# Maxima per half of the keys, the next context split in eight pieces, and the probabilities' low part in thirds, in a two-attention program on one core

## What is computed

```
x = x + tanh(g_xattn[0]) * L0_xattn(layernorm(x), ctx, ctx, Wq, Wk, Wv, Wo)   # 16 heads
x = x + tanh(g_ffn[0])   * L0_ffn(layernorm(x), w1, conv_w, conv_b, w2)
x = x + tanh(g_xattn[1]) * L1_xattn(layernorm(x), ctx, mask, Wq, Wkv, Wo)     # 8 heads
x = x + tanh(g_ffn[1])   * L1_ffn(layernorm(x), w_gate, w_up, w_down)
# an attention: q, k, v by projection; softmax(q k / sqrt(d)) v per head; projection
```

## Time and profile before

| | us |
|---|---|
| median of 3 runs | 2538.94 (2537.11 to 2543.28) |
| profiled execution, its own time | 2547.8 |
| its span, first to last instruction | 2546.0 |
| first attention | about 0 to 850 |
| first feed-forward | about 850 to 1210 |
| second attention | about 1210 to 2005 |
| second feed-forward | about 2005 to 2546 |

### The profile page before, as it was taken

How to read it: one execution, slowest core, us unless ns; L and a number is a source line. 1 busy time by engine, 2 the same in 40 slices (tenths; PEclk the granted TensorE clock), 3 DMA queues, 4 the chain that set the end, 5 groups by cost and what they waited for, 6 DMA issues and landing times. The chain is left out here.

```text
span 2546.0 us, 42229 instructions
## 1 busy us (share of the span) xinstructions
PE 2015.1 (79%) x15208; PEld 1408.1 (55%) x15208; DVE 1553.7 (61%) x2829; ACT 976.9 (38%) x1305; POOL 998.9 (39%) x706
## 2 busy tenths in 40 slices
PE   3678887887888578888388999899889522799997
PEld 2455665665666367777245666666667412344443
DVE  3655656656654388787543554554454398788883
ACT  2155555655657663233213444443444311111111
POOL 4044444544546621212211222222222376566662
PEclk8898998998997689999698999999999755899998
DMA  4232232232321320101332333233331210000100
GB/s 152 56 88 71 84 91 80 79 94 66 85 79 36 117 64 23 43 22 36 128 100 74 100 86 102 77 104 100 86 104 55 89 62 16 17 31 31 36 22 29
DMA packets 152278, 179.25 MB, mean 70 GB/s; under 512 B 60456, under 2 KB 120104, under 8 KB 151592
## 3 DMA queue, kind: packets, MB, share of 16 engines
q1 hardware_dynamic: 152104, 176.86, 24.1%
HBM read 129.96 MB, written 46.60 MB: 69 GB/s over the span
## 5 line engine op out<-in xcount | busy, mean ns | idle before, releaser
L549 POOL TENSOR_TENSOR a_p_hl<-a_p,a_p_hl 125x1344 bf16<-125x1344 f32 x192 | 525.0, 2735 | 962.8 <-ACT a_p_hl L647 962.3
L875 PE MATMUL a_psum<-a_chl,a_w 128*128 128x375 bf16 x1536 | 308.5, 358 | 55.9 <-DVE a_chl L722 45.3
L964 PE MATMUL a_psum<-a_k_st,a_q_st 96*112 96x375 bf16 (+2 forms) x1024 | 259.1, 346 | 111.5 <-DVE a_nm L782 64.7
L647 ACT ACTIVATE a_p_hl<-a_p 125x1344 bf16<-125x1344 f32 x192 | 254.0, 1323 | 125.1 <-PE a_psum L982 122.1
L637 ACT ACTIVATE a_p<-a_psum 125x1344 f32<-125x1344 f32 x192 | 247.9, 1291 | 135.5 <-PE a_psum L944 132.1
L875 PE MATMUL a_psum<-a_w,a_chl 128*125 128x512 bf16 x1152 | 268.1, 382 | 1.6 <-DVE a_xnT L752 0.9
L782 DVE TENSOR_REDUCE a_nm<-a_psum 112x1 f32<-112x750 f32 x256 | 236.1, 930 | 53.5 <-PE a_psum L964 51.2
L875 PEld LDWEIGHTS a_psum<-a_chl,a_w 128*128 128x128 bf16 x1536 | 159.4, 107 | 179.8 <-issue 92.6
L944 PE MATMUL a_psum<-a_q_st,a_k_st 99*125 99x224 bf16 (+2 forms) x1536 | 227.9, 272 | 4.2 <-ACT a_p L637 4.2
L964 PEld LDWEIGHTS a_psum<-a_k_st,a_q_st 96*112 96x112 bf16 (+2 forms) x1024 | 108.3, 132 | 195.6 <-DVE a_nm L782 85.1
L982 PEld LDWEIGHTS a_psum<-a_v_st,a_p_hl 125*128 125x128 bf16 x4608 | 183.4, 100 | 39.7 <-issue 23.5
(11 more groups left out here) (223 smaller groups left out, 3331.5 us busy)
## 6 DMA issues: line engine op xcount, KB each, us to landing
a_k_st<-a_k SPq DMA_DIRECT2D x192, 187.5 KB, 3.4
a_c<-in_ctx_t SPq DMA_DIRECT2D x32, 750.0 KB, 5.4
a_k<-a_k_tmp SPq DMA_DIRECT2D x64, 375.0 KB, 3.0
a_q_st<-a_q SPq DMA_DIRECT2D x192, 56.0 KB, 2.9
a_q<-a_q_tmp SPq DMA_DIRECT2D x64, 112.0 KB, 1.9
x<-a_xo SPq DMA_DIRECT2D x32, 224.0 KB, 2.3
f_w<-in_w1T SPq DMA_DIRECT2D x4, 1024.0 KB, 10.4
f_w<-in_w2T SPq DMA_DIRECT2D x4, 1024.0 KB, 16.8
```

The source lines that it names most:

```text
L549: nc.gpsimd.tensor_tensor(p_hl[0:MC, h % 2, 1, :], p32[0:MC, h % 2, :], p_hl[0:MC, h % 2, 0, :], ALU.subtract).then_inc(plo_done, 1)
L647: nc.scalar.activation(p_hl[0:MC, par, 0, :], p32[0:MC, par, :], ACT.Copy).then_inc(phi_done, 1)
L875: ins = nc.tensor.matmul(out, lhs, rhs, start=(c == 0 and n == 0), stop=(c == KC - 1 and n == 2))
L964: ins = nc.tensor.matmul(sm_[0:HALF, kh, 0:MK], q_stack(b.parity, at(h), rows)[:, s * HALF:(s + 1) * HALF], k_stack(b.parity, at(h), rows) ...
```

## The change

In the first attention only (`stacked`):

- The units of quarter 3 stand in slots 0, 2, 4, 8, 10 instead of 0, 2, 6, 8, 12.
- `scores` waits and signals per half of the keys (one bank each); VectorE takes two reductions of 375 elements into `nm_half`, and per group of 8 heads one minimum of the two into `nm`, for which M waits (nm_done).
- ScalarE copies half 0 of row b+2's context after K(3,1) in quarter 2 and half 1 at the head of quarter 3. VectorE splits each half in four pieces of 128 x 375, (quarter, place) by the table `CHUNKS`, place 2j behind the first maximum of head j and 2j+1 behind the second. SP loads half 1 after Q3 of quarter 2 instead of at the head of quarter 3.

In both attentions:

- SP regroups the keys as soon as they are sent and have arrived (`regroup`, semaphore k_sent), and the queries likewise (q_sent), instead of both after Q.
- GpSimd's low part is three instructions of 125 x 448 with one signal behind the third.

```diff
+        if units and units[0][0] == "X" and stacked:
+            at = [0, 2, 4, 8, 10]
...
-        kq_sent = sem("kq_sent")
+        k_sent, q_sent = sem("k_sent"), sem("q_sent")
...
+            def regroup(b, cc, n_done, sent, tmp, dram, stack, width, parts):
                 sp.wait_ge(unit_done, n_done)
+                sp.dma_start(dram[cc].rearrange("a p n -> p a n"), tmp[:, cc % 2, :, :]).then_inc(sent, 16)
                 n_used = value((b.index - 1) * H + (cc + 1) * HC)
+                n_sent = value((b.index * KC + cc + 1) * 16)
                 if b.number is None or b.number >= 2:
                     settle()
                     sp.wait_ge(st_ready, n_used)
+                sp.wait_ge(sent, n_sent)
...
                 if kind == "K" and k[1] == 1:
-                    send_k(k[0], value(n))
+                    regroup(b, k[0], value(n), k_sent, k_tmp, k_dram, k_st, M, (0, 1, 0))
                 elif kind == "Q":
-                    send_q_and_regroup(b, k, n)
+                    regroup(b, k, value(n), q_sent, q_tmp, q_dram, q_st, S, (0, 0, 1))
...
-                if q == 3:
+                if q == 3 and not stacked:
                     if (b + 2).exists():
                         load_ctx(b + 2, 1)
...
                     after_unit(unit)
+                    if stacked and unit[:2] == ("Q", KC - 1) and (b + 2).exists():
+                        load_ctx(b + 2, 1)
...
-                        nc.gpsimd.tensor_tensor(p_hl[0:MC, h % 2, 1, :], p32[0:MC, h % 2, :],
-                                                p_hl[0:MC, h % 2, 0, :], ALU.subtract).then_inc(plo_done, 1)
+                        for n in range(3):
+                            cols = slice(n * 2 * S, (n + 1) * 2 * S)
+                            ins = nc.gpsimd.tensor_tensor(p_hl[0:MC, h % 2, 1, cols], p32[0:MC, h % 2, cols],
+                                                          p_hl[0:MC, h % 2, 0, cols], ALU.subtract)
+                        ins.then_inc(plo_done, 1)
...
                 if q == 3 and (b + 2).exists():
-                    split_ctx(b + 2, 0, units.base + units.k)
+                    split_ctx(b + 2, 1 if stacked else 0, units.base + units.k)
...
+                def unit_step(unit):
+                    unit_hi_part(unit)
+                    if stacked and unit[:2] == ("K", (KC - 1, 1)) and (b + 2).exists():
+                        split_ctx(b + 2, 0, None)
...
+            def split_chunk(b, kh, c):
+                cols = slice(kh * MK, (kh + 1) * MK)
+                if c == 0:
+                    dve.wait_ge(ctx_hi, b.index * 2 + kh + 1)
+                ins = nc.vector.tensor_tensor(chl[:, 1, c, cols], c32[:, c, :], chl[:, 0, c, cols], ALU.subtract)
+                if c == KC - 1:
+                    ins.then_inc(ctx_split, 1)
...
+                if stacked:
+                    n = (b.index * H + h) * 4 + s * 2
+                    for kh in range(2):
+                        dve.wait_ge(sm_ready, n + kh + 1)
+                        nc.vector.tensor_reduce(nm_half[:, kh, s, h:h + 1], sm_[0:HALF, kh, 0:MK], AX.X, ALU.max,
+                                                negate=True).then_inc(sm_done, 1)
+                    if s == 1 and (h + 1) % H2 == 0:
+                        heads = slice(h + 1 - H2, h + 1)
+                        dve.wait_ge(sm_done, n + 2)
+                        nc.vector.tensor_tensor(nm[:, :, heads], nm_half[:, 0, :, heads], nm_half[:, 1, :, heads],
+                                                ALU.min).then_inc(nm_done, 1)
+                    return
...
+            CHUNKS = {(2, 3): [(0, 0)], (2, 4): [(0, 1)], (2, 5): [(0, 2)], (2, 6): [(0, 3)],
+                      (3, 1): [(1, 0)], (3, 2): [(1, 1)], (3, 3): [(1, 2), (1, 3)]}
...
+                if stacked:
+                    at = terms[0][0](h)
+                    for kh in range(2):
+                        if b.number != 0:
+                            pe.wait_ge(sm_done, n * 2 + kh - 1)
+                        elif n >= 3:
+                            pe.wait_ge(sm_done, n * 2 + kh - 5)
+                        nc.tensor.matmul(sm_[0:HALF, kh, 0:MK],
+                                         q_stack(b.parity, at, 96)[:, s * HALF:(s + 1) * HALF],
+                                         k_stack(b.parity, at, 96)[:, kh * MK:(kh + 1) * MK],
+                                         start=True, stop=True).then_inc(sm_ready, 1)
+                    return
```

More of the change, by code:

```diff
@@ L207, in cross_attention @@
         nm = sb("nm", [HALF, 2, H], F32)
+        if stacked:
+            nm_half = sb("nm_half", [HALF, 2, 2, H], F32)
+            nm_done = sem("nm_done")
         m_parts = sb("m_parts", [H2, 2, 3, S], BF16)
@@ L338, in _ @@
             units = Units()
-            n_sent = Units(KC)
             def value(v):
@@ L417, in send_q_and_regroup @@
                     sp.wait_ge(st_ready, n_used)
[L418 to L424, removed]
+                sp.wait_ge(sent, n_sent)
+                for (row, col), part in zip(((0, 0), (32, 0), (64, 0)) if stacked else ((0, 0), (64, 0), (0, 8)), parts):
+                    c0 = col + cc * HC
+                    sp.dma_start(stack[row:row + DK, b.parity, c0 * width:(c0 + HC) * width].rearrange(
+                        "p (h n) -> p h n", h=HC), dram[cc, part].rearrange(
+                        "(h p) n -> p h n", h=HC)).then_inc(st_in[cc], 16)
             def move_maxima(b, g, n_done):
@@ L594, in unit_hi_part @@
                 kind, k, b = unit
-                if unit[:2] == ("K", (0, 0)) and b.number != 0:
+                if unit[:2] == ("K", (0, 0)) and (b.number == 1 or not stacked and b.number != 0):
                     split_ctx(b, 1, None)
@@ L669, in quarter @@
                 slots = slots_of(q, b)
+                def unit_step(unit):
+                    unit_hi_part(unit)
+                    if stacked and unit[:2] == ("K", (KC - 1, 1)) and (b + 2).exists():
+                        split_ctx(b + 2, 0, None)
                 for j in range(HC):
                     for unit in slots[4 * j]:
-                        unit_hi_part(unit)
+                        unit_step(unit)
                     if b.exists():
@@ L815, in quarter, with unit_step, next_context @@
             def quarter(q, b):
-                if q == 3 and (b + 2).exists():
-                    split_ctx(b + 2, 0)
                 slots = slots_of(q, b)
+                def unit_step(unit):
+                    unit_lo_part(unit)
+                def next_context(at):
+                    if stacked and (b + 2).exists() and (q, at) in CHUNKS:
+                        for kh, c in CHUNKS[q, at]:
+                            split_chunk(b + 2, kh, c)
                 for j in range(HC):
                     h = q * HC + j
+                    if q == 3 and j == 0 and not stacked and (b + 2).exists():
+                        split_ctx(b + 2, 0)
                     for k in (0, 1):
                         for unit in slots[4 * j + k]:
-                            unit_lo_part(unit)
+                            unit_step(unit)
                     preparing = q == 2 and (b + 2).exists()
@@ L836, in quarter @@
                     for unit in slots[4 * j + 2]:
-                        unit_lo_part(unit)
+                        unit_step(unit)
                     if (b + 1).exists():
                         maximum(b + 1, h, 1)
+                    next_context(2 * j + 1)
                     for unit in slots[4 * j + 3]:
-                        unit_lo_part(unit)
+                        unit_step(unit)
                 for unit in last_unit(q, b):
                     unit_lo_part(unit)
+            CHUNKS = {(2, 3): [(0, 0)], (2, 4): [(0, 1)], (2, 5): [(0, 2)], (2, 6): [(0, 3)],
+                      (3, 1): [(1, 0)], (3, 2): [(1, 1)], (3, 3): [(1, 2), (1, 3)]}
             def enter(i):
@@ L891, in unit_products @@
                 if kind == "M":
-                    pe.wait_ge(sm_done, (b.index * H + (k + 1) * H2) * 2)
+                    if stacked:
+                        pe.wait_ge(nm_done, b.index * 2 + k + 1)
+                    else:
+                        pe.wait_ge(sm_done, (b.index * H + (k + 1) * H2) * 2)
                 if kind == "OP" and k == 0:
```

13 lines of the change are left out of this document (3 added, 10 removed).

## The result

The changed kernel takes 2576.01 us (median of four runs, 2571.16 to 2577.64) against 2541.11 us (four runs, 2537.11 to 2543.76): a ratio of 1.0129, 95% interval 1.0107 to 1.0151. It is slower by some 35 us, past the forecast range. The profiled span grew from 2546.0 to 2575.6 us, at a mean granted clock of 0.892 (before 0.900).

A forecast was written before the change was run, and what follows sets the result against it. TensorE was taken to idle for VectorE's maxima (55.2 us) and context split (17.7 us). Six rounds +12.0, seventh -0.9, prologues +2.0 and +3.9, second attention -9.2, thirds +1.0: +8.8, 2547.8 to 2556.6 us; range 2517 to 2567.

The forecast's parts named there:

- the likeliest case: Whole kernel: slower as the terms sum, +8.8 us, between 2536 and 2560 us; chance 0.45.
- A: First attention's rounds, last score product of quarter 2 to second of head 12: +2.7 us from ScalarE's wait for the load.
- B: First attention's quarter 3, second score product of head 12 to key product K(0,1): K(0,1) +3.1 us late, 2.7 included.
- I put that maximum 0.3 us earlier: VectorE's maximum before context piece (2,6), at 396.65 in the old trace: 0.3 us earlier, ending at 397.3.
- Rival C: Quarter 3: second context load late or pieces blocked by GpSimd, 1.5 to 2.8 us in six rounds, 2557 to 2565; chance 0.15.
- The 0.45 us for GpSimd: Quarter 3, VectorE's context pieces before K(0,1): waiting for GpSimd's instruction costs 0.45 us, ends 0 and 0.95.
- Stacks, rounds: First attention's rounds: regrouping keys and queries apart gives -0.6 us a round; the 3.15 us query wait mostly stays.
- its regrouping starts about 2 us later: Both prologues: queries sent soon after keys are regrouped about 2 us later, with TensorE waiting; +3.9 us over both.
- Second attention, rounds: Second attention: regrouping apart removes TensorE's six waits for queries, -9.2 us, ends -9.2 and 0.
- Halves: First attention, two reductions per maximum: 0.06 us more each, prologue +2.0 us, quarters 0 and 1 -0.5 us a round.
- Rival B: First attention: 80 waits for maxima, 55.2 us, go, giving 36 us; 2518 us, or 2533 with half; chance 0.30.
- Thirds: GpSimd's low part: two more instruction starts per head, felt only in five TensorE waits; +1.0 us, ends 0 and 2.0.

The follow-up runs named there:

- stacks_alone: The kernel before with keys and queries regrouped apart in both attentions and nothing else: 2546.75 us, ratio 1.0008.
- all_but_context: The changed kernel with the context handled as before, old slots included; halves, thirds and stacks apart stay: 2535.34 us, ratio 0.9956.
- context_alone: The kernel before with only the context's moved copies, eight pieces, later load and new quarter 3 slots: 2578.22 us, ratio 1.0132.
- context_two_buffers: context_alone with one context buffer per half in the first attention, both loads at the head of quarter 2: 2542.76 us, ratio 0.9997.

## Why the prediction was wrong

The direction was that of the likeliest case; the size was not, 35 us measured against 8.8. The stand of ScalarE was foreseen, and in the round shown A and B came out nearly as priced. Three steps failed: what stands before the load, the prologues, and the gains elsewhere in the round, which do not add to the moved context.

- **Context, A.** The mechanism was right: ScalarE's copy waits for a load that cannot start before piece (2,6). Predicted +2.7, measured +3.1 (5.9 to 9.0). The landing, taken as 5.0, was 4.7 to 5.2 in the six rounds. The step that failed is "I put that maximum 0.3 us earlier": the piece was to end 0.2 us after ScalarE comes free, and ended 0.9 to 2.0 us after it. What stands before the piece got slower. VectorE's normalisation, two instructions of one source, starts beside GpSimd's: it took 2.57 us for two at 410.61, under GpSimd's six thirds from 409.69 to 416.43, and 1077 ns each in the mean of all rounds instead of 539. The groups of 190 to 800 us, first before, then after:

```profile
L714 DVE TENSOR_SCALAR a_xn<-a_xin,a_mv,a_root 112x512 f32<-112x512 f32 x12 | 6.0, 539 | 0.0
```

```profile
L719 DVE TENSOR_SCALAR a_xn<-a_xin,a_mv,a_root 112x512 f32<-112x512 f32 x12 | 12.5, 1077 | 0.0
L735 DVE TENSOR_TENSOR a_chl<-a_c,a_chl 128x375 bf16<-128x375 f32 x48 | 29.5, 624 | 0.0
```

  So ScalarE stood 7.0 us in that round, not 5.3. The slow normalisation also delays the score product at which A begins, which waits 2.82 us where before it waited 1.63; that part of the price lies in the rest of the round. Rival C named the point from which it decides, a wait over six us, but the load was not late, its place was, and C's price was too small.
- **Context, B.** Predicted +0.4 beyond A, measured +1.2. In the round shown B is 10.01 us, as the steps had it (10.05). But they were set against the one round of the earlier trace rows, whose B, 9.64 us, is longer than the mean of 9.28, while the mean after is 10.5. The 0.45 us for GpSimd was some 0.3: of the two pieces before K(0,1) the last took 1.37 us in two of six rounds, and 0.54 in the others.
- **Stacks, rounds.** Right in kind: six waits for queries of 2.8 us remain, and in the second attention they fell from 9.2 us to 4.0.
- **Stacks, prologue.** The failed step is "its regrouping starts about 2 us later": I priced the last group alone, 2 us in each attention. All four groups are delayed through the two k_tmp buffers: the fourth group's keys are sent at 75.96 us instead of 70.21. At the first wait for queries it is 6.6 and 8.1 us, where the maxima and the stacks were to cost 2.0 and 3.9 together. How much of the delay is left by then varies: stacks_alone has 8.5 us in the first prologue and all_but_context, with the same queue, 1.7. Second prologues without the split take 117.3 to 121.5 us over the runs, with it 125.6 to 126.9, and before has one of the shortest.
- **Second attention, rounds.** Predicted -9.2, measured -8.3. The size fits, the reason only in part: TensorE's waits for queries fell by 5.2, and all_but_context, with the same queue, is just 2.0 us faster there. Part of the fit is luck.
- **Halves.** 0.06 us more per maximum, from 5.16 us for six: 12 halves take 5.53 us: right, and by the Trainium skill's fixed cost (VectorE: DVE Perf Modes, The TRN2 errata) it would have been 0.125. But the prologue's +2.0 drawn from it was wrong: alone the halves cost nothing there. Their gain in the rounds, predicted as 0.5 a round, is 1.6 alone. Rival B was right that the waits for maxima go, 55.2 to 29.5 us, and far off with its 36 us, the kernel with halves alone being 0.23% faster: longer waits for queries and 5.4 us more busy time in five rounds take part of it back.
- **Thirds.** Predicted +1.0, alone -0.48%, some 12 us: the sign was wrong. I looked for who waits for GpSimd, and the gain sits with who is blocked by it: VectorE's split, 2.70 and 3.01 us, and through it K(0,1). Of the 2.4 us that a round gains, A and B show 1.1; where the rest of it comes from was not traced. The price of the cut was right in kind, GpSimd's waits in the changed kernel being 11.0 us in 12 pieces instead of 6.5 in five.
- **The sum.** Terms did not add. With the context left where it was, the other three give 0.9956; beside the moved context they give nothing (1.0129 against 1.0132). The table shows where: without the moved context they take 0.7 us from A, 0.4 from B and 1.6 from the rest, beside it 0.2, 0.4 and nothing, where the prediction had 1.1 outside A and B. TensorE's busy and idle time says more: from context_alone to after, idle time falls by 12.8 us in five rounds and busy time grows by 9.9. Halves alone, too, turn 13.7 us less idle time into 5.4 more busy time, at an unchanged clock; here the clock fell besides, from 0.90 to 0.89, where thirds alone raised it. My sum priced the slower clock for one product a round. Why the other parts do not lift the clock beside the moved context was not tested further, and stays open.

The miss in the span is 29.6 less 8.8, 20.8 us. The first attention's rounds cost 23 instead of 11.1, which is 12 of it: a round grew by 4.1 instead of 2.0, and of the difference 0.4 lies in A, 0.8 in B and 0.8 in the rest. The prologues' 14.7 instead of 5.9 are another 8.8, and the second attention's 0.9 less gained is set against the 1.0 that the thirds were to cost apart. The medians lie further apart, by 34.9, because the profiled execution of before stood above its own median.

The Trainium skill (GPSIMD Engine Reference, Key points) describes the sharing as contention with two kinds of VectorE instructions: those with two SBUF inputs, and those in a 2-port perf mode. The runs agree on the first kind by the split (2.85, 2.15, 1.87 us with GpSimd's instruction whole, in thirds, in sixths). The normalisation, whose one tensor input lies in SBUF, is held as well. Two of its instructions with 512 columns take 0.99 us together by themselves, no longer than two pieces with 375 (1.00), which would fit the second kind; no view here names the mode.

## What to carry to other kernels

Before a copy is moved to an earlier place in an engine's order, follow its buffer round the whole ring (last reader, queue, landing): an engine that works in order stands for the difference, with all that is queued behind. Price an instruction on GpSimd also by what VectorE cannot do during it, and cut it into a few where VectorE has work that it blocks. A reorder of SyncE's queue that helps where keys and queries are far apart costs two trips in a row where they are close, so ask it of each stage by itself.

## What the runs showed of the hardware

- A VectorE instruction that is held by a GpSimd subtraction in flight ends a fixed time after that one's end: the split of 1500 f32 columns from SBUF 1.58 us after it in 24 of 24 cases, with GpSimd's instruction whole and in thirds (mean durations 2850 and 2145 ns; with sixths 1870), a piece of 375 columns 0.41 us, the normalisation of 512 columns 0.28 (all six held ones in context_alone), a minimum of 16 columns 0.03. The normalisation goes from 539 to 1077 ns in the mean, the minimum from 0.18 us to as much as 2.3.
- The holding goes the other way too. In context_two_buffers, 190 to 800 us, nine of GpSimd's 100 subtractions have a whole VectorE piece of 0.54 us inside them that was not held; these nine last 3.65 to 3.95 us, the other 91 from 2.72 to 2.89.
- A GpSimd subtraction of 125x448 takes 1.04 us, of 125x224 0.64, of 125x1344 2.73: cutting costs some 0.2 us a piece.
- VectorE's reductions of 375 columns from PSUM, 537 ns each, follow each other every 0.46 us (12 in 5.53 us).
- TensorE stood 2.82 and 3.61 us within 12 us (410.9 to 422.6 us; granted clock 0.50 from 413 to 423); the 12 products behind took 3.70 us, at a clock of 0.56, where 12 at a clock of 1.00 took 2.07 in the kernel before.
